# A mixture-of-experts kernel: two of six result fetches moved into the expert loop, and the final sum shared out anew among VectorE, TensorE and GpSimd

## What is computed

```python
x = hidden_states.reshape(-1, 256)                    # 1024 tokens
router_logits = x @ gate_w.T                          # 64 experts
probs = softmax(router_logits)
topk_w, topk_idx = jax.lax.top_k(probs, 6)            # six experts a token
topk_w = topk_w / sum(topk_w)
h = silu(einsum('th,eih->tei', x, experts_w1))        # 176 hidden columns
y = einsum('tei,ehi->teh', h, experts_w2)
routed_out = einsum('teh,te->th', y, combine)         # the six results, weighted
shared_out = (silu(g) * u) @ shared_down.T
# and around the layer: x = x + layernorm(routed_out + shared_out)
```

## Time and profile before

| what | us |
|---|---|
| median of 3 runs | 296.32 |
| lowest, highest | 295.72, 297.56 |
| span of the profiled execution | 294.5 |
| median less that span | 1.8 |
| TensorE busy in that span | 242.7 |
| VectorE busy | 174.5 |
| GpSimd busy | 129.8 |

### The profile page before, as it was taken

The page is one execution under the profiler, slowest core; times in us unless marked ns, Lnnn a source line. Parts: engine busy times, 40 slices in busy tenths (PEclk is TensorE's granted clock), DMA queues, the critical chain, the costliest instruction groups (busy, mean ns, idle before and its releaser), DMA issues.

```text
span 294.5 us, 4193 instructions
## 1 busy us (share of the span) xinstructions
PE 242.7 (82%) x1379; PEld 175.8 (60%) x1379; DVE 174.5 (59%) x542; ACT 80.8 (27%) x181; POOL 129.8 (44%) x163
## 2 busy tenths in 40 slices
PE   6658979980596679978859999899999999985990
PEld 6323658540253435666648888788888777632780
DVE  4438897989978756512444888533444444358084
ACT  2383582293002401242101121023322311200033
POOL 7008500006777477671702666555555775610000
PEclk9995999997599859999959999999999999997998
DMA  7999999932333133456896999999899232589313
GB/s 220 346 377 372 370 381 421 417 155 80 105 120 119 61 120 121 125 177 179 277 409 215 344 308 377 379 379 377 296 355 386 99 108 73 177 299 367 141 36 107
DMA packets 34615, 72.00 MB, mean 244 GB/s; under 512 B 4576, under 2 KB 24608, under 8 KB 34080
## 3 DMA queue, kind: packets, MB, share of 16 engines
q1 hardware_dynamic: 29024, 55.68, 53.9%
q0 software_dynamic: 5568, 16.03, 14.7%
HBM read 44.89 MB, written 26.80 MB: 243 GB/s over the span
## 4 chain that ended last, share of the span: by engine, by line
PE 51%; DVE 23%; DMA 15%; issue 5%; ACT 3%; SPq 1%; POOL 1%; ACTq 0%; DVEq 0%; POOLq 0%
DMA early<-x_slots 9%; PE bank L898 8%; PE bank L872 8%; PE bank L691 6%; PE bank L894 5%; PE bank L739 4%; PE bank L882 4%; DVE stats L1016 4%; PE bank L726 4%; PE bank L915 3%; PE bank L699 3%; DMA y_rows<-zbuf,token_i 3%; PE bank L981 2%; DMA w_all<-y_rows 2%; PE bank L953 2%
## 5 line engine op out<-in xcount | busy, mean ns | idle before, releaser
L530 POOL DMA_INDIRECT y_rows<-zbuf,token_i x66 | 64.2, 973 | 58.7 <-DVE zbuf L1340 46.5
L509 POOL DMA_INDIRECT x_slots<-rows,slot_i x48 | 47.4, 988 | 48.7 <-DVE slot_i L1169 33.8
L1340 DVE COPY zbuf<-bank 128x256 f32<-128x256 f32 x66 | 24.9, 419 | 50.4 <-PE bank L898 49.4
L647 ACT ACTIVATE sgu_sb<-bank 128x256 f32<-128x256 f32 x33 | 12.7, 383 | 95.2 <-PE bank L882 95.2
L739 PE MATMUL bank<-x2nT,sgu_sb 128*128 128x512 f32 (+1 forms) x48 | 26.2, 695 | 11.1 <-DVE nt L1274 10.8
L872 PE MATMUL bank<-work,w_all 128*128 128x128 f32 x256 | 33.7, 285 | 1.7 <-DVE work L1324 1.7
L1324 DVE COPY work<-bank 128x512 f32<-128x512 f32 x33 | 22.4, 683 | 18.9 <-PE bank L915 18.9
L872 PEld LDWEIGHTS bank<-work,w_all 128*128 128x128 f32 x256 | 32.0, 201 | 2.3 <-issue 2.2
L898 PE MATMUL bank<-w_all,sgu_sb 128*128 128x256 f32 x128 | 33.0, 396 | 0.0
L898 PEld LDWEIGHTS bank<-w_all,sgu_sb 128*128 128x128 f32 x128 | 22.7, 190 | 8.9 <-issue 6.6
L915 PE MATMUL bank<-ident,early 128*128 128x128 f32 x128 | 18.6, 278 | 7.4 <-DMA early<-x_slots 6.5
(11 more groups left out here) (202 smaller groups left out, 368.7 us busy)
## 6 DMA issues: line engine op xcount, KB each, us to landing
w_all<-pairs SPq DMA_DIRECT2D x32, 752.0 KB, 9.4
x_slots<-hidT SPq DMA_DIRECT2D x8, 1152.0 KB, 12.6
early<-x_slots SPq DMA_DIRECT2D x64, 144.0 KB, 6.6
w_all<-y_rows SPq DMA_DIRECT2D x4, 1024.0 KB, 6.6
w_all<-y_rows SPq DMA_DIRECT2D x4, 512.0 KB, 9.0
y_rows<-zbuf,token_i POOLq DMA_INDIRECT x66, 5.8
x_sb<-x SPq DMA_DIRECT2D x4, 256.0 KB, 3.5
out<-work SPq DMA_DIRECT2D x4, 256.0 KB, 2.1
```

The costliest lines, as they stand in the source:

```text
L509: pool.indirect_dma_start(x_slots, bass.IndirectOffsetOnAxis(ap=slot_i[:, c, k:k + 1], axis=0), rows[:, c, :], None).then_inc(sent_first[u ...
L530: pool.indirect_dma_start(y_rows, bass.IndirectOffsetOnAxis(ap=token_i[:, s % 32:s % 32 + 1].bitcast(U32), axis=0), yS[:, s % 8, :], None) ...
L1340: dve.tensor_copy(yS[:, s % 8, :], y_b[s % 4][:, 0:C]).then_inc(y_done, 1)
```

## The change

- The extra pair moves from block 56 to block 44 (`X0 = E - 20`). `position(e)` gives the block of expert e.
- Choice 5 is taken as complete after expert 53 (block 55) and choice 4 after expert 57 (block 59). SyncE fetches both then, and the other four each on its own: choice 3 after block 62, choice 2 after 63, choice 1 after 64, choice 0 in four pieces after 65.
- A token whose lowest expert is above 53, or whose second lowest is above 57, would break this. VectorE marks such tokens (`find_late`), TensorE counts them with one more matmul, and VectorE adds them, times three, to the number that raises the fallback's flag.
- VectorE sums choices 5, 4, 3 and 2 into `part`: half of choice 5 in each of the last two turns of the loop, choice 4 after the loop, 3 and 2 after the flag's branch. TensorE sums choices 1 and 0 and adds `part`.
- The five filler matmuls before the sum are gone; of the ten after the loop nine are left.
- The residual adds of the first three rounds go to GpSimd; the last one stays on VectorE.

```diff
-    X0 = E - 8
+    X0 = E - 20
+        late = sb("late", [P, 2, NT], BF16)
+        late_no = sb("late_no", [P, 1])
+        part = rows[:].rearrange("p n w -> p (n w)")[:, 0:NT * C].rearrange("p (c d) -> p c d", c=NT)
-        LOW = TOPK // 2
+        LOW = 2
...
+        def position(e):
+            return e if e < X0 else e + EXTRA
+        EARLY = (E - 11, E - 7)
+        def complete(k):
+            return position(EARLY[TOPK - 1 - k] if k >= 4 else E - 1 - k)
...
             for s in range(E - 8):
-                sp.wait_ge(token_done, s // 2 + 1)
+                sp.wait_ge(token_done, position(s) // 2 + 1)
...
+            def landed(first, k):
+                for s in range(first, complete(k) + 1):
+                    sp.wait_ge(scat[s % 8], scattered(s))
+            landed(complete(5) - 7, 5)
+            sp.dma_start(ya[5], yr[:, 5]).then_inc(ya_in[5], 16)
+            landed(complete(5) + 1, 4)
+            sp.dma_start(ya[4], yr[:, 4]).then_inc(ya_in[4], 16)
...
-            for s in range(NB - TOPK - 8, NB - TOPK):
-                sp.wait_ge(scat[s % 8], scattered(s))
-            for k in range(TOPK)[::-1]:
-                s = NB - 1 - k
-                sp.wait_ge(scat[s % 8], scattered(s))
-                if k >= 2:
-                    sp.dma_start(ya[k], yr[:, k]).then_inc(ya_in[k], 16)
+            for k in (3, 2, 1):
+                landed(complete(k + 1) + 1, k)
+                sp.dma_start(ya[k], yr[:, k]).then_inc(ya_in[k], 16)
+            landed(complete(1) + 1, 0)
             for p in range(4):
-                sp.dma_start(yb[:, :, 2 * p:2 * p + 2, :], yr[:, 0:2, 2 * p:2 * p + 2, :]).then_inc(yb_in[p], 16)
+                sp.dma_start(ya[0][:, 2 * p:2 * p + 2, :], yr[:, 0, 2 * p:2 * p + 2, :]).then_inc(yb_in[p], 16)
...
+            for p in range(3):                                   # GpSimd, after its last scatter
+                cs = slice(2 * p, 2 * p + 2)
+                pool.wait_ge(norm_act, 14 + 2 * p)
+                pool.tensor_tensor(work[:, cs, :], work[:, cs, :], x_sb[:, cs, :], ALU.add).then_inc(fin_pool, 1)
...
             def counts():                                        # TensorE
+                pe.wait_ge(late_done, 1)
+                pe.matmul(count_b[:, E:E + 2 * NT], ones[:], late[:].rearrange("p k c -> p (k c)"), start=True, stop=True)
...
-            KEEP = 10
+            KEEP = 9
...
-            pe.wait_ge(ya_in[LOW], 16)
-            for _ in range(KEEP // 2):
-                pe.matmul(h_b[0][:], ident[:], x2nT[:, 0, 0:T], start=True, stop=True)
-            pe.wait_ge(ya_in[2], 16)
+            pe.wait_ge(ya_in[1], 16)
             for c in range(NT):
-                add_rows(2, c, ya[2][:, c, :])
+                add_rows(1, c, ya[1][:, c, :])
             for p in range(4):
                 pe.wait_ge(yb_in[p], 16)
                 for c in (2 * p, 2 * p + 1):
-                    for k in (1, 0):
-                        mm = add_rows(k, c, yb[:, k, c, :])
+                    mm = add_rows(0, c, ya[0][:, c, :])
...
+            def find_late():                                     # VectorE, after place(2)
+                mark(dve.tensor_scalar(late[:, 0, :], topk[:, :, 5], float(SPAN * (EARLY[0] + 1)), None, ALU.is_gt))
+                settle()
+                dve.tensor_scalar(late[:, 1, :], topk[:, :, 4], float(SPAN * (EARLY[1] + 1)), None, ALU.is_gt
+                                  ).then_inc(late_done, 1)
...
+                link(dve.tensor_reduce(late_no[:], count_b[:, E:E + 2 * NT], AX.X, ALU.add))
+                link(dve.scalar_tensor_tensor(late_no[:], late_no[:], float(EXTRA + 1), upto[:, E - 1:E], ALU.mult, ALU.add))
...
+            def add_high(k, cs):
+                if k == 5:
+                    dve.wait_ge(dn_cp, 4)
+                    dve.wait_ge(wk_done, 1)
+                dve.wait_ge(ya_in[k], 16)
+                for c in cs:
+                    mark(dve.scalar_tensor_tensor(part[:, c, :], ya[k][:, c, :], wk[:, c, k:k + 1],
+                                                  work[:, c, :] if k == 5 else part[:, c, :], ALU.mult, ALU.add))
+                settle()
...
                 take_output(t - 1)
+                if t >= NP - 2:
+                    add_high(5, range(TB * (t - NP + 2), TB * (t - NP + 3)))
             take_output(NP - 1)
+            add_high(4, range(NT))
...
-            for k in range(LOW, TOPK)[::-1]:
-                dve.wait_ge(ya_in[k], 16)
-                for c in range(NT):
-                    mark(dve.scalar_tensor_tensor(work[:, c, :], ya[k][:, c, :], wk[:, c, k:k + 1], work[:, c, :],
-                                                  ALU.mult, ALU.add))
-                settle()
+            for k in (3, 2):
+                add_high(k, range(NT))
...
                 variances(2 * p, 2)
-                if p:
-                    final_add(p - 1)
                 sharpen(8 + p, 2 * p, 2)
-            final_add(3)
+            dve.wait_ge(norm_act, 20)
+            dve.tensor_tensor(work[:, NT - 2:NT, :], work[:, NT - 2:NT, :], x_sb[:, NT - 2:NT, :], ALU.add
+                              ).then_inc(fin_dve, 1)
```

More of the change, by code:

```diff
@@ L90, in moe_block @@
         rows = sb("rows", [P, NT, W])
+        part = rows[:].rearrange("p n w -> p (n w)")[:, 0:NT * C].rearrange("p (c d) -> p c d", c=NT)
         w_all = sb("w_all", [P, 2 * RING, PW])
         w_flat = w_all[:].rearrange("p j w -> p (j w)")
-        LOW = TOPK // 2
-        ya = [w_flat[:, NT * C * n:NT * C * (n + 1)].rearrange("p (c d) -> p c d", c=NT) for n in range(TOPK)]
-        yb = w_flat[:, 0:2 * NT * C].rearrange("p (k c d) -> p k c d", k=2, c=NT)
+        LOW = 2
+        ya = [w_flat[:, NT * C * n:NT * C * (n + 1)].rearrange("p (c d) -> p c d", c=NT) for n in range(TOPK)][::-1]
         def scan_part(n, k):
@@ L230, in moe_block @@
         scat = [sem(f"scat{j}") for j in range(8)]
-        ya_in = {k: sem(f"ya_in{k}") for k in range(2, TOPK)}
+        ya_in = {k: sem(f"ya_in{k}") for k in range(1, TOPK)}
         yb_in = [sem(f"yb_in{p}") for p in range(4)]
+        late_done = sem("late_done")
         wk_done = sem("wk_done")
@@ L951, in add_rows @@
             def add_rows(k, c, rows):
-                return pe.matmul(in_sum(c), diag[:, c, k, :], rows, start=(k == 2 and c % 2 == 0),
+                return pe.matmul(in_sum(c), diag[:, c, k, :], rows, start=(k == 1 and c % 2 == 0),
                                  stop=(k == 0 and c == 1))
@@ L987, in _ @@
                 for c in (2 * p, 2 * p + 1):
-                    for k in (1, 0):
-                        mm = add_rows(k, c, yb[:, k, c, :])
+                    mm = add_rows(0, c, ya[0][:, c, :])
                 if p:
                     pe.wait_ge(high_done, 1)
-                    pe.matmul(in_sum(2 * p), ident[:], work[:, 2 * p, :], start=False, stop=False)
-                    mm = pe.matmul(in_sum(2 * p + 1), ident[:], work[:, 2 * p + 1, :], start=False, stop=True)
+                    pe.matmul(in_sum(2 * p), ident[:], part[:, 2 * p, :], start=False, stop=False)
+                    mm = pe.matmul(in_sum(2 * p + 1), ident[:], part[:, 2 * p + 1, :], start=False, stop=True)
                 mm.then_inc(sum_ps, 1)
@@ L1362, in _ @@
                 take_output(t - 1)
+                if t >= NP - 2:
+                    add_high(5, range(TB * (t - NP + 2), TB * (t - NP + 3)))
             take_output(NP - 1)
+            add_high(4, range(NT))
             with dve.If(dve.value_load(ext_i[0:1, 2 * EXTRA:2 * EXTRA + 1], min_val=0, max_val=1)):
                 dve.wait_ge(dn_cp, 4)
-                dve.tensor_copy(nt0[:, 0:1], nt0[:, 0:1]).then_inc(o_y, 1)
+                dve.tensor_copy(part, work[:]).then_inc(o_y, 1)
                 with dve.Fori(0, E) as e:
@@ L1371, in _ @@
                         dve.wait_ge(o_y_ps, e * NT + c + 1)
[L1372 to L1373 removed]
+                        dve.scalar_tensor_tensor(part[:, c, :], y_b[0][:, 0:C], cw[:, c, bass.ds(e, 1)],
+                                                 part[:, c, :], ALU.mult, ALU.add).then_inc(o_y, 1)
                 dve.wait_ge(o_y, E * NT + 1)
[L1376 to L1383, removed]
[L1384 to L1389 removed]
+            for k in (3, 2):
+                add_high(k, range(NT))
             dve.tensor_copy(nt0[:, 0:1], nt0[:, 0:1]).then_inc(high_done, 1)
@@ L1394, in _ @@
                     link(dve.tensor_tensor(work[:, 0:2, :], sum_b[0][:].rearrange("p (c d) -> p c d", c=2),
-                                           work[:, 0:2, :], ALU.add))
+                                           part[:, 0:2, :], ALU.add))
                 stats_of(in_sum if p else in_work, (2 * p, 2 * p + 1))
                 variances(2 * p, 2)
-                if p:
-                    final_add(p - 1)
                 sharpen(8 + p, 2 * p, 2)
-            final_add(3)
+            dve.wait_ge(norm_act, 20)
```

(2 more changed lines are left out.)

11 lines of the change are left out of this document (8 added, 3 removed).

## The result

The changed kernel is slower: the ratio to the kernel before is 1.0059, 95% interval 1.0032 to 1.0087, some 1.7 us, over 20 runs of each. The medians of all runs are 298.82 and 296.36 us, 2.5 us or 0.8% apart. The ratios and intervals in this document leave out the runs that are over 1.5% above the fastest of their kernel, and so can differ by up to 0.7% from the ratio of the medians. The forecast was 294.0, 0.8% faster. The profiled execution took 301.02 us, 2.2 above its median; part of its length is luck, as the first experiment shows, so stages are compared here, not its whole.

What follows compares the result with a forecast made beforehand. TensorE was taken to bound the loop, then a chain of scatter, fetches, fillers and sum. First round at 274.9 plus rounds of 17.3 gives 292.2 against 294.5, 2.3 us less: 294.0 us from 296.3, range 290.4 to 298.3.

Steps and rivals of the forecast that it cites:

- 5.12 from the last to the end: End of the rounds: 5.12 us from the last refinement to the program's end, part of 17.3 us for the rounds.
- the mis-sized lead: Start of the rounds: first round ready at 274.9 us against 279.6, 4.6 us earlier.
- The blocked refinements: Rounds: GpSimd's add blocks VectorE's next refinement; three rounds of 3.3 us, 17.3 us in all against 14.96 before.
- Rival 1: Rounds: GpSimd's adds don't block; rounds take 14.1 us, time 290.8 us; chance 0.27.
- The fetches: After the loop: block 62 lands sooner, so choice 3's fetch starts at 257.8 us instead of 262.3.
- the time from choice 3's fetch to choice 1's landing: Fetches after the loop: about 11 us, bounds 9.8 and 11.7, so choice 1 lands at 268.8.
- the sum to the first round: TensorE's sum: 5.1 us for choice 1, 0.9 for choice 0 and 0.1 more, from choice 1's landing.
- Rival 2: Fetches get no lead: choice 3 starts at 262.3 us as before, time 298.5 us; chance 0.14.
- Choice 5 inside the loop: Last turns of the loop: fetched from 244.2 us, added without holding up scatters; free, but the tightest cover.
- Routing and the extra pair: Routing and loop: the added work hides; 0 us taken for both together, bounds -0.3 and +0.8.
- a sign of a missed price: Loop's end: must come within 1 us of 255.3, or the extra pair's new place has a missed price.
- rival 3: Sum: clock stays at 1.2 GHz throughout, every matmul 0.86 us, time 297.1 us; chance 0.06.

Runs made afterwards that it cites:

- the first experiment: The changed kernel run once more, unaltered, for a second profile: ratio to the kernel before 1.015, median 299.25 us.
- late_memset: Changed kernel with all residual adds on VectorE, plus one unread GpSimd memset after ScalarE's last normalisation: ratio to the kernel before 1.009.
- one_gpsimd: Changed kernel with only the first round's residual add on GpSimd, the other three on VectorE: ratio to the kernel before 0.9969.
- wait_only: Changed kernel with all residual adds on VectorE; GpSimd only waits for ScalarE's last normalisation before leaving: ratio to the kernel before 1.0146, median 298.46 us.
- none_early: Changed kernel with all residual adds on VectorE, choices 5 and 4 fetched only after blocks 60 and 61: ratio to the kernel before 1.003.
- extra_late: Changed kernel with the extra pair back at block 56: ratio to the kernel before 1.0141.
- warm_sum: Changed kernel with all residual adds on VectorE and sixteen fillers after the loop instead of nine: ratio to the kernel before 0.9828, median 290.65 us.

## Why the prediction was wrong, point by point

- **The step that failed** is in the rounds: "5.12 from the last to the end", which took over the end of the kernel before unseen. I moved work onto GpSimd and asked what it does beside VectorE, but not when GpSimd may leave. Leaving takes it 8.0 us, so a GpSimd that works until 2.4 us before the last add ends is the last to be done: 5.6 us behind the end of VectorE's last add instead of 2.5. Counted from where the last refinement is no longer blocked (291.12), the term of 5.12 measured 8.2. The sum is then: -2.3 forecast, +3.0 for the closing wait, +1.7 for a lead of 2.9 and not 4.6, -0.7 for the rounds, makes +1.7. So the closing wait alone turns a gain of 2.3 us into a loss of 0.7, and the mis-sized lead, less what the rounds gave back, did the rest. No rival had the wait. It is shown by late_memset, one_gpsimd and wait_only.
- **The blocked refinements** came as forecast, one in each of three rounds. Size: 14.1 us from the first round to the end of the last add, 14.8 forecast, since a blocked round was 3.1 us and not 3.3. The Trainium skill ("SBUF — State Buffer", section "SBUF: two separate sides") calls the shared port an exclusive lock, with the loser fully blocked. The rows agree: 0.16 us became 1.04 to 1.12, ending with GpSimd's add. Rival 1 is out.
- **The fetches.** Block 62 landed 3.3 us behind its issue, 3.5 forecast: right, and none_early shows the cause, since there it is 8.0. The term that was too small is the time from choice 3's fetch to choice 1's landing, 12.4 us against 11, above both bounds given for it (9.8 and 11.7; by its bytes alone it would be 9.6, three quarters of the 12.8 from 262.3 to 275.1). SyncE could issue choice 1 only at 265.93, since it waited for block 63 and then for block 64, caught behind choices 3 and 2; I had let only block 65 be caught. And the sum to the first round took 6.7 us against 6.1, with 4 us at 1.2 GHz and not 3.4. Together the lead was 2.9 us, not 4.6. The seven profiles have 11.4 to 13.8 us for the first term and 6.0 to 7.5 for the second, and none reaches a lead of 4.6. Rival 2, no lead at all, did not come, though the smallest lead, 1.0 us in wait_only, is near it.
- **Choice 5 inside the loop** was free, as forecast. Its fetch started 10.9 us ahead of the first filler, where the forecast had 244.2 and 255.1. VectorE never waited for it; its copy at 256.59 led to the scatter at 257.29 as that at 253.63 did to 254.32 before, 0.7 us in both. Block 64 went out 2.8 us behind block 62 and not 2.5, since GpSimd's issue of block 63 took 1.23 us and not 0.96; the last copy, 0.7 us late where 0.8 was forecast, was done in time.
- **Routing and the extra pair** at 0. The loop ended 2.9 us late in the first profile, which the prediction called a sign of a missed price; extra_late and the spread of the twelve profiles show no such price for the pair, though they would miss one below a microsecond. The routing's part wasn't tried alone, so its 0 is not shown.
- **The clock through the sum** (rival 3): it came back after 4 us. What it cost on the way, 2.1 us (6.7 less the 4.6 of warm_sum), was in the sum with 1.7, four matmuls at 0.86 and not 0.43, but that more fillers behind the loop take it away was no part of the change. Whether the five fillers it removed would have done the same wasn't tried.

## What to carry to other kernels

Before work is moved to an idle engine, ask three things: what it blocks while it works, who waits for it, and how long that engine needs to leave the program; the last shows only as a wait at the end line. A part of a change that loses can hide one that gains: here fetching early was worth 1.0% and was buried under adds that cost 1.5 to 2% (1.015 against 0.9933, and 1.0193 alone; 1.8 and 1.5% by the medians). Filler matmuls paid best here where they end just as the data land, 16 against 9 or 20, so try their number anew when a fetch is moved. And a difference of a microsecond between two profiles says little when two profiles of the same kernel differ by 3 (spans 299.3 and 296.1): compare stages, over as many profiles as there are.

## What the runs showed of the hardware

GpSimd takes 8.0 to 8.1 us from the end of its instructions to the end of the program, in six profiles with a last add, memset or wait at six different times; why so long stays open. The wait for it is booked on TensorE's sequencer. In the kernel before, the scatters of blocks 58, 59 and 61 landed in 2.4 us, with no 1 MB fetch under way when they were issued (that of block 54, also without one, in 4.3). A scatter landed in 8.0 us when it was issued 0.7 us behind one 1 MB fetch and just ahead of a second, in 4.8 when issued 1.1 us behind a single fetch, and in 3.3 when issued 3 us behind one. In the last three pairs of scatters of the changed kernel, while VectorE adds choices 5 and 4, GpSimd's issue of the second of each pair takes 1.2 us, that of the first 0.96 though the same adds run beside it; in none_early, without adds there, the same second issue takes 0.97. So it goes with the adds, but why only every second one is not shown. One such row of the changed kernel's timeline:

```profile
258.56 1.23 POOL L554 DMA_INDIRECT y_rows<-zbuf,token_i  x1 [0.30 <-issue]
```

The loop's end moves by 6 us over the twelve profiles, 1.6 us between two of the same kernel; it is earlier in those whose granted clock from 44 to 60 us is 1.00, as counted under the first experiment.
